# One more tile shape in a post-norm decoder layer: p's transposes by row halves, the attention sum kept in PSUM, and a new order on TensorE, VectorE and ScalarE

## What is computed

```python
def _L0_attn_ref(x, W_Q, b_Q, W_K, b_K, W_V, b_V, W_O, b_O):
    Q, K, V = (jnp.einsum('btd,hkd->bthk', x, W) + b for W, b in ...)
    attn = softmax(jnp.einsum('bqhk,bshk->bhqs', Q, K) / sqrt(64))
    out_h = jnp.einsum('bhqs,bshk->bqhk', attn, V)
    return jnp.einsum('bqhk,hdk->bqd', out_h, W_O) + b_O
def _L0_xattn_ref(query, key, value, Wq, bq, Wk, bk, Wv, bv, Wo, bo):
    q, k, v = (... reshape(b, s, 16, 64))
    attn = softmax(jnp.einsum('bshd,bsgd->bshg', q, k) / sqrt(64))
    out = jnp.einsum('bshg,bsgd->bshd', attn, v)
    return transpose(out, (0, 2, 1, 3)).reshape(b, -1, 1024) @ Wo.T + bo
x = _layernorm(x + _L0_attn_ref(x, ...))
x = _layernorm(x + _L0_xattn_ref(x, ctx_1024, ctx_1024, ...))
x = _layernorm(x + _L0_ffn_ref(x, ...))
```

## Time and profile before

| | us |
|---|---|
| median of 3 runs | 406.34 |
| lowest, highest | 406.04, 407.11 |
| the profiled execution | 407.05 |
| its span | 405.2 |

### The profile page before, as it was taken

The page is one execution under the profiler, slowest core; times in us unless marked ns, Lnnn a source line. Parts: engine busy times, 40 slices in busy tenths (PEclk is TensorE's granted clock), DMA queues, the critical chain, the costliest instruction groups (busy, mean ns, idle before and its releaser), DMA issues.

```text
span 405.2 us, 15945 instructions
## 1 busy us (share of the span) xinstructions
PE 394.5 (97%) x6580; PEld 343.2 (85%) x6580; DVE 286.9 (71%) x662; ACT 240.5 (59%) x814; POOL 146.7 (36%) x223
## 2 busy tenths in 40 slices
PE   8999999999999999999999999999999999999995
PEld 7797788788888888788888888888988888898985
DVE  4685786865758687866849678676848778687645
ACT  5685664745666584745567475645558566555552
POOL 0541444331523354331413454422415454323314
PEclk9999999999999999999999999999999999999999
DMA  7900112210110213110110213100101111211001
GB/s 244 371 27 8 43 25 63 65 37 2 33 31 11 46 29 91 37 28 8 32 25 15 49 29 92 34 21 8 42 15 24 41 39 23 47 39 26 27 28 52
DMA packets 43758, 19.33 MB, mean 48 GB/s; under 512 B 36592, under 2 KB 41200, under 8 KB 43696
## 3 DMA queue, kind: packets, MB, share of 16 engines
q1 hardware_dynamic: 42880, 16.88, 16.1%
q0 software_dynamic: 528, 1.45, 1.0%
q10 hardware_dynamic: 288, 0.07, 0.1%
HBM read 8.95 MB, written 1.05 MB: 25 GB/s over the span
## 4 chain that ended last, share of the span: by engine, by line
PE 85%; DVE 6%; SPq 3%; issue 2%; ACT 2%; DMA 1%; POOL 0%; POOLq 0%; DVEq 0%
PE ps L1223 7%; PE ps L1168 7%; PE ps L1048 7%; PE ps L1076 7%; PE ps L1148 7%; PE ps L1127 6%; PE ps L1136 6%; PE ps L1028 5%; PE ps L1030 4%; PE ps L1029 4%; PE ps L1178 4%; PE ps L1067 3%; SPq L317 3%; PE ps L1104 3%; PE ps L1162 2%; PE ps L1156 2%
## 5 line engine op out<-in xcount | busy, mean ns | idle before, releaser
L541 ACT ACTIVATE p<-ps,neg_max 128x128 f32<-128x128 f32 x256 | 90.3, 385 | 40.8 <-DVE neg_max L807 40.8
L414 POOL TENSOR_TENSOR p<-p,row_inv 128x1024 f32<-128x1024 f32 x32 | 60.7, 1898 | 60.2 <-DVE row_inv L813 60.2
L534 ACT ACTIVATE pt<-ps 128x512 f32<-128x512 f32 x62 | 34.3, 624 | 48.6 <-PE ps L1127 48.5
L541 ACT ACTIVATION_READ_ACCUMULATOR p<-ps,neg_max 128x1 f32 x256 | 57.9, 226 | 0.0
L807 DVE TENSOR_REDUCE neg_max<-ps 128x4 f32<-128x512 f32 x64 | 41.6, 673 | 4.8 <-PE ps L1223 4.0
L753 DVE TENSOR_TENSOR ot<-ps,bv 128x512 f32<-128x512 f32 x32 | 22.0, 689 | 27.6 <-PE ps L1148 27.5
L1136 PE MATMUL ps<-x1t,wq 128*64 128x64 f32 x1024 | 33.8, 224 | 1.6 <-DVE v2s L763 0.9
L1127 PE MATMUL ps<-ident,p 128*128 128x128 f32 x256 | 34.6, 279 | 0.8 <-POOL p L414 0.8
L1223 PE MATMUL ps<-kt,qt 64*64 64x128 f32 x1024 | 35.2, 275 | 0.0
L1136 PEld LDWEIGHTS ps<-x1t,wq 128*64 128x64 f32 x1024 | 31.5, 138 | 3.0 <-issue 1.9
L1168 PE MATMUL ps<-wo,ot 128*128 128x128 f32 x256 | 32.7, 281 | 0.6 <-DVE ot L753 0.6
(11 more groups left out here) (152 smaller groups left out, 835.5 us busy)
## 6 DMA issues: line engine op xcount, KB each, us to landing
v<-v2s SPq DMA_DIRECT2D x256, 32.0 KB
xg<-x_t SPq DMA_DIRECT2D x4, 256.0 KB, 2.9
cg<-ctx_t SPq DMA_DIRECT2D x4, 256.0 KB, 3.4
wo<-w_o SPq DMA_DIRECT2D x2, 512.0 KB, 9.5
xres<-x_nat SPq DMA_DIRECT2D x15, 64.0 KB, 1.8
pt<-w_qk SPq DMA_DIRECT2D x3, 256.0 KB, 4.3
out<-x2b SPq DMA_DIRECT2D x3, 256.0 KB, 2.3
x2b<-w_v SPq DMA_DIRECT2D x1, 512.0 KB, 7.3
```

The source lines that it names most:

```text
L414: nc.gpsimd.tensor_tensor(ph, ph, row_inv[:, 8 * half:8 * half + 8].unsqueeze(2).to_broadcast([T, 8, T]), ALU.mult).then_inc(p_ready, 1)
L534: nc.scalar.activation(pt[:, u * BANK:(u + 1) * BANK], bank(T_BANK[u]), ACT.Copy).then_inc(pt_ready, 1)
L541: last = nc.scalar.activation(p[:, hd * T:(hd + 1) * T], bank(S_BANK[q])[:, pos * T:(pos + 1) * T], ACT.Exp, bias=neg_max[:, hd:hd + 1], a ...
```

## The change

- p's transposes go by rows: each head's 128x128 transpose becomes two, of rows 0 to 63 and 64 to 127, each into its own bank; all sixteen of eight heads are one block, and the two banks are signalled at its end. `pt_part` puts the halves back together when ScalarE copies them.
- TensorE's order: cross values right behind p2's transposes, then the second eight heads' scores, then the cross sum; x1's transpose and the first transposes of p come before the cross queries, x2's transpose after the cross output.
- `t1` is no longer a tile of its own: the sum is written over the output projection's bank 4. The cross sum, which writes to that bank, waits for x1 in place of the sum. x1's and x2's transposes go to banks 2 and 1.
- VectorE: the first inverse sums between the two block-diagonal products; both read-outs of cross values ahead of the maxima; the regrouping ahead of both query read-outs in phases 0 to 2 and behind both in phase 3.
- ScalarE: the regrouping ahead of the third quarter of the exponentials, x2's copy at the end of the step. GpSimd: x1 with its bias added behind the first division of p.
- Start: the first weight slice has 256 columns, and the third unit of the first block is written out with its own waits; the split of the up-projection's weights goes to ScalarE and to step 2.

```diff
@@ -170,7 +169,7 @@
         V2, O, PT2, PV2, Q2, O2, S2 = [2, 3], 4, 5, [4, 5], [2, 3], 2, 4
-        X1T, X2T = 7, 0
+        X1T, X2T = 2, 1
         BLOCK_BANKS = {blk: [2, 3, 4, 5] for blk in "ABCDEF"}
@@ -194,6 +193,14 @@
             return c // 2, c % 2
+        def pt_part(u):
+            half, e = u // 2, u % 2
+            return (pt[:, half * 8 * T:(half + 1) * 8 * T].rearrange("p (h e q) -> p e h q", h=8, e=2)[:, e],
+                    bank(T_BANK[u]).rearrange("p (h q) -> p h q", h=8))
+        t1 = bank(O, D)
         def ot2_half(k2):
@@ -279,7 +286,7 @@
             return not isinstance(s, int) or FIRST_LOOPED <= s <= LAST_LOOPED
-        QK_PARTS = [slice(0, 128), slice(128, BANK)] + [slice(u * BANK, (u + 1) * BANK) for u in range(1, 4)]
+        QK_PARTS = [slice(0, 256), slice(256, BANK)] + [slice(u * BANK, (u + 1) * BANK) for u in range(1, 4)]
         HALVES = [slice(0, BANK), slice(BANK, 2 * BANK)]
@@ -406,13 +422,12 @@
                     rstd1(s, b_par)
-                for half in range(2):
-                    if a:
-                        pool.wait_ge(inv_ready, 2 * s + half + 1)
-                        ph = p[:, half * 8 * T:(half + 1) * 8 * T].rearrange("q (h k) -> q h k", h=8)
-                        nc.gpsimd.tensor_tensor(ph, ph, row_inv[:, 8 * half:8 * half + 8].unsqueeze(2).to_broadcast([T, 8, T]),
-                                                ALU.mult).then_inc(p_ready, 1)
+                if a:
+                    over_sum(s, 0)
+                if bc:
+                    x1_biased(s, b_par)
+                if a:
+                    over_sum(s, 1)
                 if d:
@@ -531,7 +547,8 @@
                     act.wait_ge(mm_t, 4 * s + u + 1 if u < 2 else 4 * s - 4 + u + 1)
-                    nc.scalar.activation(pt[:, u * BANK:(u + 1) * BANK], bank(T_BANK[u]), ACT.Copy).then_inc(pt_ready, 1)
+                    dst, src = pt_part(u)
+                    nc.scalar.activation(dst, src, ACT.Copy).then_inc(pt_ready, 1)
                 def exponentials(q):
@@ -589,8 +606,8 @@
                     nc.scalar.activation(x1t[:], bank(X1T, T), ACT.Copy).then_inc(x1t_ready, 1)
-                if not static or s > 2:
-                    x2_transposed(s - 1, X2T)
+                if d:
+                    regrouped(s)
                 if a:
@@ -603,10 +620,11 @@
                     f_high(0)
-                if d:
-                    regrouped(s)
                 if a:
                     exponentials(3)
+                if static and s == 2:
+                    act.wait_ge(wup_scaled, 2)
+                    nc.scalar.activation(wup_hi[:], wup, ACT.Copy).then_inc(wup_split, 1)
                 if static and s == 0:
@@ -617,12 +635,15 @@
                     qk_out(g + 1, "A")
+                if not static or s > 2:
+                    x2_transposed(s - 1, X2T)
             run_steps(act, step)
...
                 act.wait_ge(mm_t, 4 * (B - 1) + u + 1)
-                nc.scalar.activation(pt[:, u * BANK:(u + 1) * BANK], bank(T_BANK[u]), ACT.Copy).then_inc(pt_ready, 1)
+                dst, src = pt_part(u)
+                nc.scalar.activation(dst, src, ACT.Copy).then_inc(pt_ready, 1)
             exp2(B)
@@ -766,9 +787,9 @@
                 dve.wait_ge(xres_ready, s)
-                nc.vector.tensor_tensor(t1[:], bank(O, D), xres[b_par][:], ALU.add).then_inc(sum1_ready, 1)
+                nc.vector.tensor_tensor(t1, bank(O, D), xres[b_par][:], ALU.add).then_inc(sum1_ready, 1)
                 dve.wait_ge(sum1_ready, s)
-                nc.vector.bn_stats(st1[:], t1[:]).then_inc(stats1_ready, 1)
+                nc.vector.bn_stats(st1[:], t1).then_inc(stats1_ready, 1)
                 dve.wait_ge(bq_scaled, 1)
@@ -852,6 +873,9 @@
                     block_diagonal(s, 0)
+                if a and bc:
+                    inverse_sums(0)
+                if d:
                     block_diagonal(s, 1)
@@ -871,17 +895,14 @@
                     return
-                if a:
-                    inverse_sums(0)
-                    score_max(2)
                 if bc:
...
                     values2_out(s, 0, d)
+                    values2_out(s, 1, d)
                 if a:
+                    score_max(2)
                     score_max(3)
-                if bc:
-                    values2_out(s, 1, d)
                 if phase == 3 and not static:
@@ -889,16 +910,19 @@
                         dve.wait_ge(in_own_j, 16)
+                    if d and phase < 3:
+                        regrouped(s)
                     q2_out(s, 0)
-                if d:
-                    regrouped(s)
-                if bc:
+                    if static and s == 1:
+                        inverse_sums(1)
                     q2_out(s, 1)
+                    if d and phase == 3:
+                        regrouped(s)
                 if phase == 0 and a and bc:
...
                     qk_out(g + 1, "A")
-                if a:
+                if a and not (static and s == 1):
                     inverse_sums(1)
@@ -914,8 +938,7 @@
                     nc.vector.tensor_scalar(wup[:, FH:FP], wup[:, FH:FP], gam[:, 0:1], D ** 0.5, ALU.mult, ALU.mult).then_inc(wup_scaled, 1)
-                    dve.wait_ge(wup_scaled, 2)
-                    nc.vector.tensor_copy(wup_hi[:], wup).then_inc(wup_split, 1)
+                if static and s == 2:
                     dve.wait_ge(wup_split, 1)
@@ -1117,15 +1140,18 @@
                 last.then_inc(mm_y, 1)
-            def transpose_p(n, u):
-                if u % 2 == 0:
-                    pe.wait_ge(p_ready, 2 * n + u // 2 + 1)
-                for i in range(4):
-                    hd = 4 * u + i
-                    last = nc.tensor.transpose(bank(T_BANK[u])[:, i * T:(i + 1) * T], p[:, hd * T:(hd + 1) * T], ident[:])
-                last.then_inc(mm_t, 1)
+            def transpose_p(n, half):
+                pe.wait_ge(p_ready, 2 * n + half + 1)
+                for i in range(8):
+                    hd = 8 * half + i
+                    for e in range(2):
+                        rows = slice(HALF * e, HALF * e + HALF)
+                        mm = nc.tensor.transpose(bank(T_BANK[2 * half + e])[:, i * HALF:(i + 1) * HALF],
+                                                 p[rows, hd * T:(hd + 1) * T], ident[rows, rows])
+                        if i == 7:
+                            mm.then_inc(mm_t, 1)
             def project_q2(s, u):
@@ -1234,14 +1260,21 @@
                     nc.tensor.matmul(bank(FIRST_BANKS[0]), wqk_hi[:, 0:128], xg_lo[:], start=False, stop=True).then_inc(mm_qk, 1)
+                    project_qk(0, "A", lambda r: None, FIRST_BANKS, units=(1,))
+                    pe.wait_ge(w_hi, 2)
+                    nc.tensor.matmul(bank(FIRST_BANKS[2]), wqk_hi[:, 256:384], xg_hi[:], start=True, stop=False)
+                    nc.tensor.matmul(bank(FIRST_BANKS[2]), wqk_hi[:, 256:384], xg_lo[:], start=False, stop=False)
                     pe.wait_ge(w_lo, WQK_SPLIT[0])
-                    project_qk(0, "A", lambda r: None, FIRST_BANKS, units=(1, 2, 3))
+                    nc.tensor.matmul(bank(FIRST_BANKS[2]), wqk_lo[:, 256:384], xg_hi[:], start=False, stop=True).then_inc(mm_qk, 1)
+                    project_qk(0, "A", lambda r: None, FIRST_BANKS, units=(3,))
                     pe.wait_ge(w_lo, WQK_SPLIT[1])
...
                 if bc:
-                    transpose_p(s - 1, 2)
-                    transpose_p(s - 1, 3)
+                    if s > 3:
+                        pe.wait_ge(xnt_ready, s - 3)
+                    transpose_p(s - 1, 1)
                 if phase == 0 and a and bc:
@@ -1283,13 +1316,6 @@
                     transpose_p2(s)
-                if static and s == 0:
-                    read(1, (0, "D"))
-                    read(3, (0, "D"))
-                if a:
-                    scores(1)
                 if bc:
@@ -1299,32 +1325,27 @@
                         values2(u, own)
+                if static and s == 0:
+                    read(1, (0, "D"))
+                    read(3, (0, "D"))
+                if a:
+                    scores(1)
+                if d:
+                    pe.wait_ge(v2_moved, 16 * 16 * (s - 1))
+                    if bc:
+                        pe.wait_ge(x1_ready, s)
+                    weighted_v2(s, 0)
+                    weighted_v2(s, 1)
+                if bc:
                     if static and s == 1:
                         pe.wait_ge(in_perm, 16)
-                    if a:
-                        pe.wait_ge(exp_ready, 4 * s + 1)
+                    pe.wait_ge(v2s_ready, 2 * s - 1)
                     pe.wait_ge(x1_ready, s)
                     nc.tensor.transpose(bank(X1T, T), x1[:], perm[:]).then_inc(mm_x1t, 1)
-                    if late:
-                        if a:
-                            pe.wait_ge(exp_ready, 4 * s + 2)
-                        transpose_x2(s - 1, X2T)
-                if d:
```

(28 more changed lines are left out.)

19 lines of the change are left out of this document (11 added, 8 removed).

## The result

| | before | after |
|---|---|---|
| median | 406.48 us (4 runs) | 418.14 us (4 runs) |
| lowest, highest | 406.04, 407.11 | 417.38, 420.01 |
| span of the profiled execution | 405.2 us | 415.6 us |
| TensorE's granted clock over it | 0.998 | 0.987 |

The ratio is 1.029 (95% interval 1.025 to 1.033): slower by 11.7 us, where 5.8 us faster was forecast. It lies outside the range, on its far side, and none of the slower rivals describes it. Of the four executions after, the traced one and one other have a mean granted clock of 0.987 and 0.988 and spans of 415.6 us; the other two have 0.980 and 0.981 and spans of 418.2 and 417.1 us.

A forecast was written before the change was run, and what follows sets the result against it. TensorE, busy 97% of the 405.2 us span, was taken as the bound. Three groups −2.7, step 2 +0.14, step 3 −0.83, head −2.1, tail −0.3 gave −5.8: 406.34 to 400.5 us, range 392 to 407.

The forecast's parts named there:

- Phase 3: Group's last step: TensorE's wait for the query copy behind VectorE's regrouping goes, −0.73 us; whole step −0.83.
- Step 15: Last step, counted as the third group's phase 3 step: −0.83 us, to 17.52.
- Head: Start: first slice −0.6, batch 0's transposes −0.7, step 1 −0.2, VectorE wait −0.56; together −2.1 us.
- not priced: ScalarE's strided copies of p, given no cost because the values' 1.57 us lie between transposes and the copies' readers.
- a block of halves: TensorE's sixteen row-half transposes, pairs side by side: 8 × 57 ns plus 0.18 us, 0.64 us.
- the wait for x1: New TensorE wait before the cross sum, which writes over the attention sum's bank: 0.39 us.
- the wait for p's second half: New TensorE wait for GpSimd's p before the transposes opening phases 2 and 3: about 0.5 us.
- the shorter products are eaten: Phase 2 step: new waits outweigh TensorE's shorter work, 17.71 us in place of 17.57, +0.14.
- C: Rival, chance 0.08: transpose halves do not run beside each other, 1.10 us a half block; 412.5 us.
- D: Rival, chance 0.04: a half transpose costs a whole's 105 ns, 1.25 us more a block; 438 us.
- A: Rival, chance 0.18: the new waits hardly arise, x1's chain or ScalarE's queue running half a microsecond shorter; 391.5 us.
- B: Rival, chance 0.12: PSUM reads in sum, statistics and x1 add 0.35 us in 15 steps; 405.8 us.

The follow-up runs named there:

- e1: The changed kernel with ScalarE's high split (phase 3 and step 15) moved ahead of the copy of x1's transpose: 407.28 us, ratio 1.002.
- e7: e1 with step 15's VectorE regrouping ahead of the query read-outs and its low split behind them: 404.88 us, ratio 0.996.
- e6: e5 plus a first weight slice of 256 columns and the up-projection's high split on ScalarE in step 2: 399.45 us, ratio 0.980.
- e5: e2 with VectorE's regrouping ahead of both query read-outs, but behind both in the looped phase 3: 400.19 us, ratio 0.985.
- e2: The kernel before with only p's transposes taken by row halves, and copied accordingly: 404.69 us, ratio 0.997.
- e11: The changed kernel with whole transposes put back and ScalarE's high split one exponential later: 420.65 us, ratio 1.032.
- e9: e7 with VectorE's reciprocals that release GpSimd's division of p's first half put behind x1's instruction: 408.52 us, ratio 1.003.

## Why the prediction was wrong

**"Phase 3 ... the change puts both query copies first: −0.73."** This step failed. Ahead of both copies stands a third VectorE instruction, the low split, and its input comes from ScalarE, where x1's copy now comes later and the change put the regrouping ahead of the exponentials and so ahead of the high split. The forecast had followed just this queue for p's second half ("the exponentials of the second half stay queued behind it, the regrouping too"), and not the other instruction in it. Measured in place of −0.83: +2.75 a step, 1.9 of wait and 1.55 of clock on top of what was forecast. e1 confirms it with 21.85 us.

**Step 15, priced as a phase 3 step of the third group, −0.83.** Its vector order is phase 3's, but no projections follow that cover a late regrouping. Measured +2.48; e7 takes it back (18.02, −0.33 against before).

**"Head ... together −2.1."** Measured 0.0 at the start of step 3. Batch 0's two blocks begin at 28.43 and not 28.68, 0.25 us of the 0.6 promised: the first product starts at 6.00 us in place of 5.22, 0.78 later where 0.15 was allowed. The 0.7 us for those blocks did not come at all: from their start to the values behind them it is 1.89 us now (28.43 to 30.32) and was 1.83, as the values wait 0.68 us for ScalarE's copies of p, whose two banks are signalled at a block's end. These copies are a term that the forecast put at nothing ("not priced"). From 26 us to the start of step 3 TensorE waited 2.2 us before (0.90 for cross values, 0.76 for p, 0.56 for the attention output, the one of the earlier trace rows). The last of these went as forecast, but the sum is 3.9 us now: the 0.68 us, 0.24 for x1, 0.32 for p at step 3, and in steps 1 and 2:

```profile
39.90 0.30 PE L1348 MATMUL ps<-perm,x 128*128 128x128 f32 x1 [0.59 <-DVE v2s L784]
40.92 0.71 PE L1151 MATMUL ps<-ident,p 64*128 64x64 f32 x16 [0.72 <-POOL p L410]
44.77 1.16 PE L1204 MATMUL ps<-kb,qt 64*64 64x64 f32 x64 [1.12 <-DVE qt L806]
46.19 0.71 PE L1151 MATMUL ps<-ident,p 64*128 64x64 f32 x16 [0.26 <-POOL p L410]
```

In the kernel before's order the same head gives 0.78 us (e6 against e5).

**What is left.** With both queues repaired (e7) the span is 402.6 us, where the forecast comes to 399.4 (405.2 − 5.8). Of these 3.2 us 1.8 stand at the start of step 3 (63.76 against 62.0), and the rest is about 0.1 us a step.

**Right**, by the same tables: a block of halves (0.64 us), the wait for x1 (0.34 against 0.39), the wait for p's second half (0.49 against 0.50), ScalarE idle over 2 us ahead of x1's copy (2.38), phases 0 to 2 within 0.15 us, so that "the shorter products are eaten" in phase 2. Of the rivals, C and D fall with the 0.64 us, A with the waits, and B with the 0.34 us for x1, although its read from PSUM takes 0.40 us in place of 0.34. The missing rival was a chain through the other queues of phase 3.

**What the parts are worth.** Halves: −1.9 us alone (e2), −2.9 in e1's order. Regrouping ahead of the queries: a further −4.5 (e5 against e2). The merged cross work with x1's and p's transposes ahead of the queries is no gain: e7 has it, the halves and the head, and is 5.4 us slower than e6 (phases 26.20, 23.25, 17.87, 21.84 against e6's 25.98, 22.41, 17.19, 21.61). The waits for x1 and for p (7.9 us in e7) belong to it; which share of them falls to the order and which to the bank of the sum was not taken apart further.

## What to carry to other kernels

When a change puts a wait into an engine's queue, list everything behind it until that engine is idle again, in every phase and in each written-out step, and for each the reader one engine further on; a transfer to the next group's work is as much a consumer as the value that one is thinking of. A filler that depends on nothing new (here a high split) belongs ahead of the wait. Before merging work to save changes of the array's shape, look for the shortest edit that keeps the order: here the short edits gave 7.1 us (e6), and the merged order with the same halves and head 1.6 (e7).

## What was not expected of the hardware

- A VectorE instruction on SBUF operands (128x128 float32, 0.34 us) that started 0.39 us into GpSimd's 1.90 us division took 1.59 us and ended with it; with its input in PSUM it took 0.40 us beside the same division.
- Behind waits of 1.16 to 3.25 us TensorE's clock was granted at half for some 3.5 to 7 us in some cases and not in others, in the same kernel at the same wait (e11: 0.93 and 1.00 over three steps of one form; e9: 0.55 from 42.3 to 49.9 behind 1.16 us). In e11 it did not fall with the first product after the wait: the starts go from 0.23 to 0.42 us apart only about 1 us later.

```profile
81.33 0.47 PE L1048 MATMUL ps<-xg_hi,wqk_hi 128*128 128x512 f32 x1 [2.02 <-DVE qt L803]
...
81.87 0.39 PE L1050 MATMUL ps<-xg_hi,wqk_lo 128*128 128x512 f32 x1
82.10 0.58 PE L1048 MATMUL ps<-xg_hi,wqk_hi 128*128 128x512 f32 x1
82.48 0.63 PE L1049 MATMUL ps<-xg_lo,wqk_hi 128*128 128x512 f32 x1
```
